# Six passes of a transformer kernel: seams between passes reordered, weights split by column halves, modulation partly moved into pass 0

## The reference

```
mod = silu(cond) @ Wmod + bmod               # block 0: 6 x 256 shifts and scales
h = LN(x) * (1 + sc1) + sh1;  x += attn(h @ Wqkv) @ Wos + bos          # pass 0
h = LN(x) * (1 + sc2) + sh2;  x += attn(h @ Wq, ctx @ Wk, ctx @ Wv) @ Woc + boc   # pass 1
h = LN(x) * (1 + sc3) + sh3;  x += gelu(h @ W1 + b1) @ W2 + b2         # pass 2
g = cond @ g_w + g_b, bt = cond @ b_w + b_b  # block 1: same for both norms
h = LN(x) * (1 + g1) + bt1;   x += attn(rope(h @ sa_wq), rope(h @ sa_wk), h @ sa_wv) @ sa_wo + sa_bo   # pass 3
h = LN(x) * (1 + g1) + bt1;   x += attn(rope(h @ ca_wq), rope(LN(ctx) @ ca_wk), LN(ctx) @ ca_wv) @ ca_wo + ca_bo   # pass 4
h = LN(x) * (1 + g2) + bt2;   x += gelu(h @ ff_w1 + ff_b1) @ ff_w2 + ff_b2   # pass 5
```

## Time and profile before

| what | us |
|---|---|
| median of 3 runs (4234.51 to 4236.21) | 4235.6 |
| the profiled execution | 4232.58 |
| its span | 4230.7 |
| TensorE matmuls busy | 4076.2 (96%) |
| VectorE busy | 2844.6 (67%) |
| ScalarE busy | 2746.4 (65%) |
| GpSimd busy | 2909.7 (69%) |

### The profile page before, as it was taken

The page is one execution under the profiler, slowest core; times in us unless marked ns, Lnnn a source line. Parts: engine busy times, 40 slices in busy tenths (PEclk is TensorE's granted clock), DMA queues, the critical chain, the costliest instruction groups (busy, mean ns, idle before and its releaser), DMA issues.

```text
span 4230.7 us, 95772 instructions
## 1 busy us (share of the span) xinstructions
PE 4076.2 (96%) x34870; PEld 3484.5 (82%) x34870; DVE 2844.6 (67%) x6058; ACT 2746.4 (65%) x10788; POOL 2909.7 (69%) x2714
## 2 busy tenths in 40 slices
PE   7999999999989999999999999999999999999999
PEld 6777777777779987888888888888888888888998
DVE  6888888888865556565656565777776767665443
ACT  5999999999953335666666666666666666664333
POOL 5777778888767775666565665666666666665776
PEclk9999999999999999999999999999999999999999
DMA  2110111111111212212121212322222222221110
GB/s 72 33 35 32 33 42 43 47 46 47 46 57 41 66 62 78 81 71 81 71 80 70 80 71 96 102 78 91 80 89 86 83 86 81 88 99 53 41 51 31
DMA packets 229270, 276.66 MB, mean 65 GB/s; under 512 B 37948, under 2 KB 160320, under 8 KB 228800
## 3 DMA queue, kind: packets, MB, share of 16 engines
q1 hardware_dynamic: 228732, 270.51, 18.8%
q10 hardware_dynamic: 68, 0.02, 0.0%
HBM read 85.89 MB, written 50.33 MB: 32 GB/s over the span
## 4 chain that ended last, share of the span: by engine, by line
PE 77%; POOL 10%; DVE 6%; ACT 4%; issue 3%; ACTq 0%; DMA 0%; SPq 0%; DVEq 0%; POOLq 0%
PE BANKS L580 18%; PE BANKS L582 16%; PE BANKS L581 16%; PE BANKS L768 7%; PE BANKS L732 7%; PE BANKS L720 6%; POOL PR L1194 3%; POOL Z L1236 3%; ACT PR L869 2%; PE BANKS L654 2%; PE BANKS L790 2%; POOL HL L1204 2%; DVE WL L1053 1%; POOL X L1250 1%; DVE PT L1016 1%
## 5 line engine op out<-in xcount | busy, mean ns | idle before, releaser
L1194 POOL TENSOR_TENSOR PR<-PR,RL 128x512 f32<-128x512 f32 x1024 | 1067.1, 1046 | 656.4 <-DVE RL L1021 655.8
L885 ACT ACTIVATE PR<-BANKS,NM 128x128 f32<-128x128 f32 x2048 | 729.0, 382 | 442.7 <-DVE NM L1067 440.5
L869 ACT ACTIVATE PR<-BANKS,NM 128x128 f32<-128x128 f32 x2048 | 728.4, 410 | 2.9 <-DVE NM L1009 2.8
L580 PE MATMUL BANKS<-HH,WH 128*128 128x512 f32 x1632 | 688.8, 422 | 6.4 <-DVE SN L1081 3.6
L768 PE MATMUL BANKS<-ID,PR 128*128 128x128 f32 x4096 | 624.7, 275 | 58.1 <-POOL PR L1194 28.3
L1067 DVE TENSOR_REDUCE NM<-BANKS 128x8 f32<-128x1024 f32 x256 | 313.2, 1224 | 490.8 <-PE BANKS L732 490.8
L581 PE MATMUL BANKS<-HL,WH 128*128 128x512 f32 x1632 | 643.0, 394 | 0.0
L582 PE MATMUL BANKS<-HH,WL 128*128 128x512 f32 x1632 | 642.0, 393 | 0.0
L768 PEld LDWEIGHTS BANKS<-ID,PR 128*128 128x128 f32 x4096 | 488.3, 140 | 184.0 <-POOL PR L1194 67.9
L869 ACT ACTIVATION_READ_ACCUMULATOR PR<-BANKS,NM 128x1 f32 x2048 | 514.2, 251 | 0.0
L1217 POOL TENSOR_TENSOR GL<-GF,GH 128x512 fp32r<-128x512 f32 x256 | 342.4, 1337 | 203.2 <-DVE GH L1165 203.2
(11 more groups left out here) (123 smaller groups left out, 10730.1 us busy)
## 6 DMA issues: line engine op xcount, KB each, us to landing
SW<-SN SPq DMA_DIRECT2D x1024, 128.0 KB, 2.1
x_scratch<-X SPq DMA_DIRECT2D x80, 512.0 KB, 3.2
X<-x_scratch SPq DMA_DIRECT2D x80, 512.0 KB, 4.0
CX<-in_ctx SPq DMA_DIRECT2D x32, 384.0 KB, 4.3
X<-in_x SPq DMA_DIRECT2D x16, 512.0 KB, 3.8
out<-X SPq DMA_DIRECT2D x16, 512.0 KB, 3.0
CX<-in_ctx SPq DMA_DIRECT2D x32, 128.0 KB, 4.4
STG<-in_L_xcond_W SPq DMA_DIRECT2D x4, 512.0 KB, 5.1
```

The lines of the kernel that those rows point to most:

```text
L580: e.matmul(o, lh, rh, start=first and i == 0, stop=False)
L869: made = e.activation(pr[:, r], bank[:, r], ACT.Exp, bias=nm[:, h:h + 1], accum_out=RL[npr(t)[0]][:, h:h + 1])
L885: made = e.activation(pr[:, r], bank[:, r], ACT.Exp, bias=nm[:, h:h + 1], accum_out=RL[npr(t)[0]][:, h:h + 1])
L1194: e.tensor_tensor(p3, p3, RL[npr(t)[0]][:, :].unsqueeze(2).broadcast_to([128, 4, 128]), ALU.mult).then_inc(s_nrm, 1)
```

## The change

The change has five parts.

- Prologue: modulation part 2 is made in pass 0, in two pieces of four columns at ticks TM = T0[0] + 1 and TM + 2, in bank 7, added at TM + 3 and applied at TM + 4 and TM + 5. `scores0` waits for parts 0 and 1 only, and copies to PT wait for part 2. Z of groups 0 and 1 is made on VectorE; group 1's statistics, root, Z and transposes stand at tg - 34, - 33, - 31 and from tg - 29 (before: from tg - 34, - 30, - 29 and - 24) and its Q products two ticks later. Wqkv is split one tick later.
- T0[2] and T0[5] are END[1] and END[4] (4 ticks less each), T0[3] is END[2] + 2 (one less).
- Feed forward buffers lie on AH, AL and ONES in pass 2 and on QT, KT, SN and the first V1 in pass 5. GELU waits for the last scores and not for the last transposes; exponentials of block 1 no longer wait for the end of pass 2, but `low` and V1 from the fourth on do.
- The four sums of `down` are pairs in two banks, (2, 3) for even groups and (6, 7) for odd ones. Group 1 of pass 2 is turned in banks 6 and 7.
- The weights sq, sk, sv, cq, ck, cv come by column halves of 512 with both row blocks, and products wait for their half alone. The splits of pass 4's weights stand in single ticks.

```diff
@@ T0, SOURCE
+TM = T0[0] + 1
-    T0[_p + 1] = END[_p] + {1: 4, 2: 3, 4: 4}.get(_p, 0)
+    T0[_p + 1] = END[_p] + {1: 0, 2: 2, 4: 0}.get(_p, 0)
+HALVES = ("sq", "sk", "sv", "cq", "ck", "cv")
@@ schedule
-            if kind == "a":
+            if (p, g) == (0, 1):
+                for b in range(G):
+                    at["stats", tg - 34].append(Batch(p, g, b))
+                    at["norm", tg - 31].append(Batch(p, g, b))
+                at["root", tg - 33].append((p, g))
+                turn = tg - 29
+            elif kind == "a":
...
+                    tq += 2 * ((p, g) == (0, 1))
...
-    chunks = [(T0[0] - 20, "Wqkv", 0), (T0[0] - 20, "Wqkv", 1)]
+    chunks = [(T0[0] - 19, "Wqkv", 0), (T0[0] - 19, "Wqkv", 1)]
...
-    chunks += [(e3 - 7, "cq", 0), (e3 - 7, "cq", 1), (e3 - 6, "ck", 0), (e3 - 6, "ck", 1), (e3 - 3, "cv", 0), (e3 - 3, "cv", 1),
-               (e3 + 5, "co", 0), (e3 + 5, "co", 1)]
+    chunks += [(e3 - 13, "cq", 0), (e3 - 12, "ck", 0), (e3 - 8, "cv", 0), (e3 - 6, "cq", 1), (e3 - 5, "ck", 1), (e3 - 2, "cv", 1),
+               (e3 - 1, "co", 0), (e3 + 6, "co", 1)]
@@ build: places
+            sb("HOLE0", [128, 2048], stack=first)
             AH = [sb(f"AH{i}", [128, 2, 512], R, stack=first) for i in range(2)]
             AL = [sb(f"AL{i}", [128, 2, 512], R, stack=first) for i in range(2)]
...
+            sb("HOLE1", [128, 5632], stack=gated)
+            GF[2] = [sb(f"GF{i}", [128, 512], stack=gated) for i in range(3)]
...
+        with gated2:
+            GF[5] = [sb(f"GF{i}_L1", [128, 512], stack=gated2) for i in range(3)]
@@ build: weights' old users, banks
-            w_free["cq", c] = (s_qk, 2 * 8 * NG - 1)
+            w_free["cq", c] = (s_qk, 2 * 8 * NG - 9 + 8 * c)
...
+        UP, TWO, THREE, FOUR, LATE, DOWN = (0, 1), (4, 5), (0, 1, 4), (4, 5, 6, 7), (6, 7), ((2, 3), (6, 7))
...
+            if tick == TM:
+                tp.add("modulation", (7,), s_mod, 3)
@@ SyncE
+                    if key in HALVES:
+                        name, k0 = PAIRED.get(key, (SOURCE.get(key), 0))
+                        k0 += 512 * c
+                        if key in CONTEXT:
+                            e.dma_start(stage[:, 0:512], a[name][0:128, k0:k0 + 512]).then_inc(ready, 16)
+                            e.dma_start(stage[0:64, 512:1024], a[name][128:CD, k0:k0 + 512]).then_inc(ready, 16)
+                            e.dma_start(stage[64:128, 512:1024], a[name][128:CD, k0:k0 + 512]).then_inc(ready, 16)
@@ TensorE
                 if tick == T0[0] - 20:
                     modulation(1)
-                    modulation(2)
+                if tick == TM:
+                    q.wait_ge(*tp.free("modulation"))
+                    modulation(2, 0)
+                if tick == TM + 2:
+                    modulation(2, 1)
...
-                    q.wait_ge(s_mod, 3)
+                    q.wait_ge(s_mod, 2)
...
-                    q.wait_ge(s_exp, NL0)
+                    q.wait_ge(s_exp, NL0 - 3 + min(j, 1))
...
-                        made = three(PS[(2, 3, 6, 7)[b]][:, 0:D], [(gh[:, s], gl[:, s], wh[:, j, :], wl[:, j, :])], j == 0, j == 7)
+                        made = three(PS[DOWN[g % 2][b // 2]][:, 256 * (b % 2):256 * (b % 2) + 256],
+                                     [(gh[:, s], gl[:, s], wh[:, j, :], wl[:, j, :])], j == 0 and b % 2 == 0, j == 7 and b % 2 == 1)
@@ ScalarE
-                    q.wait_ge(s_dn, 8 * NG)
+                    if m > 2:
+                        q.wait_ge(s_dn, 8 * NG)
...
-                    q.wait_ge(s_t, NL0 if p == 2 else 2 * NL0)
-                    e.activation(GF[f % 3][:, :], PS[tp.bank(("up", p, g, j))][:, :], ACT.Gelu, bias=col(WFF[p][2], j)).then_inc(s_gf, 1)
+                    q.wait_ge(*((s_s0, 16 * NG) if p == 2 else (s_s, 16 * NG)))
+                    e.activation(GF[p][f % 3][:, :], PS[tp.bank(("up", p, g, j))][:, :], ACT.Gelu, bias=col(WFF[p][2], j)).then_inc(s_gf, 1)
@@ VectorE
-                if tick == T0[0] - 11:
+                if tick == T0[0] - 12:
                     modulation(1)
+                if tick in (T0[0] - 5, T0[0] - 4):
+                    apply(tick - T0[0] + 6)
+                if tick == TM + 3:
                     modulation(2)
-                if T0[0] - 10 <= tick < T0[0] - 6:
-                    apply(tick - T0[0] + 11)
+                if tick in (TM + 4, TM + 5):
+                    apply(tick - TM - 1)
...
-                    if x.p < 2:
+                    if x.p < 2 and xq(x.p, x.g) > 1:
                         continue
```

More of the change, by code:

```diff
@@ L265, in build @@
         TB = sb("TB", [128, 4, D])
-        before, soft, gated, spare, first, second = (ExitStack() for _ in range(6))
+        before, soft, spare, first, gated, second, gated2 = (ExitStack() for _ in range(7))
         with before:
@@ L450, in build @@
                 if j == 0:
-                    for b in range(G):
-                        tp.add(("down", p, g, b), ((2, 3, 6, 7)[b],), s_res, 4 * xq(p, g) + b + 1)
+                    for i in range(2):
+                        tp.add(("down", p, g, i), (DOWN[g % 2][i],), s_res, 4 * xq(p, g) + 2 * i + 2)
         def h_of(p, g, context=False):
@@ L462, in col, with pieces, staged @@
             return COL[:, ROWS[name] + j:ROWS[name] + j + 1]
+        def pieces(buf, key, c):
+            if key in HALVES:
+                return wview(buf, key)[:, :, 512 * c:512 * c + 512]
+            rows, _, m, o = wchunk(key, c)
+            return buf[0:rows, o:o + m]
+        def staged(w, key, c):
+            rows, _, m, _ = wchunk(key, c)
+            if key in HALVES:
+                return STG[w % NSTG][:, :].rearrange("p (c n) -> p c n", c=2)
+            return STG[w % NSTG][0:rows, 0:m]
         def wchunk(key, c):
@@ L605, in project, with modulation @@
                 return e.matmul(o, HH[h][:, 1, s], wl[:, 1, cols], start=False, stop=True)
-            def modulation(part):
+            def modulation(part, half=None):
                 first, end = PARTS[part]
-                for m in range(first, end):
+                bank = PS[part if part < 2 else tp.bank("modulation")]
+                for m in range(first, end) if half is None else range(first + 4 * half, first + 4 * half + 4):
                     if m < 12:
@@ L619, in modulation @@
                         q.wait_ge(s_wgb, 64)
-                    o = PS[part][:, NB * (m - first):NB * (m - first) + NB]
+                    o = bank[:, NB * (m - first):NB * (m - first) + NB]
                     e.matmul(o, ls[0], rhs[:, 0, :], start=True, stop=False)
                     made = e.matmul(o, ls[1], rhs[:, 1, :], start=False, stop=True)
-                made.then_inc(s_mod_mm, 1)
+                if half != 0:
+                    made.then_inc(s_mod_mm, 1)
             q.wait_ge(s_ident, 16)
@@ L819, in _ @@
                         q.wait_ge(s_exp, NL0)
[L820 to L821 removed]
+                        for i in range(2):
+                            q.wait_ge(*tp.free(("down", p, g, i)))
                     for b in range(G):
                         s = slice(128 * b, 128 * b + 128)
[L824 removed]
+                        made = three(PS[DOWN[g % 2][b // 2]][:, 256 * (b % 2):256 * (b % 2) + 256],
+                                     [(gh[:, s], gl[:, s], wh[:, j, :], wl[:, j, :])], j == 0 and b % 2 == 0, j == 7 and b % 2 == 1)
                     made.then_inc(s_dn, 1)
@@ L938, in _ @@
                         q.wait_ge(*w_free[key, c])
-                    e.activation(WH[0:rows, o:o + m], STG[w % NSTG][0:rows, 0:m], ACT.Copy).then_inc(s_whi, 1)
+                    e.activation(pieces(WH, key, c), staged(w, key, c), ACT.Copy).then_inc(s_whi, 1)
         @block.vector
@@ L951, in modulation @@
                 bias = COL[:, ROWS["bmod"] + first:ROWS["bmod"] + end] if part < 2 else COL[:, ROWS[L1 + "g1_b"]:ROWS[L1 + "g1_b"] + 8]
-                e.tensor_tensor(MOD[:, first:end, :], PS[part][:, 0:NB * (end - first)].rearrange("p (m b) -> p m b", b=NB),
+                bank = PS[part if part < 2 else tp.bank("modulation")]
+                e.tensor_tensor(MOD[:, first:end, :], bank[:, 0:NB * (end - first)].rearrange("p (m b) -> p m b", b=NB),
                                 bias.unsqueeze(2).broadcast_to([128, end - first, NB]), ALU.add).then_inc(s_mod, 1)
```

77 lines of the change are left out of this document (34 added, 43 removed).

## The result

The kernel after takes 4216.5 us (median of 5 runs, 4214.0 to 4219.2); the kernel before, on the same chip, 4234.5. The ratio is 0.9960 (95% interval 0.9949 to 0.9971): faster by about 18 us, where 40 were forecast, and outside the range of 4180 to 4214. The first line is the page's busy time by engine, the others are busy time by stage as in the earlier trace rows (length, busy us and instructions of each engine, granted clock), the seams in stretches of nearly equal work before and after.

A forecast was written before the change was run, and what follows sets the result against it. TensorE and ScalarE were both taken as nearly full in passes 0 and 1, TensorE alone as the bound from 1610 us. 11 + 9 + 4 + 6 + 10 = 40 us gave 4195.6 us, range 4180 to 4214.

The forecast's parts named there:

- Its own sign of being wrong: Passes 0 and 1 over 3 us longer between first and last exponential, or a new several-us wait at an up or PV.
- Prologue: Start of the kernel: first exponential 14 us earlier, at 43, less 3 given back in pass 0; 11 us gained (4.9 to 15).
- the share given back: Pass 0: cost of modulation part 2, its addition and sets moved there, taken as 3 us (bounds nothing to 9.1).
- Seam 1/2: Between passes 1 and 2: four ticks less and earlier up products overlap the seam; 9 us gained (4 to 14).
- Seam 2/3: Between passes 2 and 3: one tick less puts the maximum ahead of two `so` splits; 4 us gained (1.5 to 6.6).
- Seam 3/4: Between passes 3 and 4: single splits hide and products wait only for their half; 6 us gained (2 to 9).
- Seam 4/5: Between passes 4 and 5: four ticks less, hidden state's transposes earlier where ScalarE has room; 10 us gained (5 to 14.7).
- (b): Rival at the seams: overlap works half, GELU chain or transposes' banks hold TensorE, clock falls again; 4210 us, chance 0.09.
- (c): Rival on VectorE: Z slowed beside GpSimd's normalization, up to 1.42 us against 0.41; 4200 us, chance 0.08.
- (d): Rival in pass 0: modulation pieces leave TensorE's clock at its lower level, 7.4 us more per batch; slower, chance 0.03.
- (e): Rival: ups wait for something ending only with pass 1, pass 0 eats the prologue's gain; no change, chance 0.03.
- (f): Rival: modulation products run at the upper clock level, part 1 taking 3.3 instead of 6.7 us; 4191 us, chance 0.04.

The follow-up runs named there:

- e8: Kernel after with modulation part 2, its addition and sets back in the prologue behind part 1; 4223.9 us, ratio 0.9971.
- e5: Kernel after with the second modulation piece, the addition and sets 3 and 4 one tick earlier; 4216.2 us over four scattered runs, ratio 0.9958.
- e1: Kernel after with the four ticks of pass 2 put back (T0[2] = END[1] + 4); 4220.1 us, ratio 0.9971.
- e13: Kernel after with statistics and Z of group 0 of passes 2 and 5 on 16 of 256 columns; 4216.2 us, one run.
- e14: Kernel after with ScalarE copying only one of four batches of group 0's hidden state per half in passes 2 and 5; 4215.3 us, one run.
- e6: Kernel after with Z of groups 0 and 1 of pass 2 on GpSimd instead of VectorE; 4223.0 us, ratio 0.9972.
- e10: Kernel after with the hidden state of pass 2's group 0 made earlier and piece by piece inside pass 1; 4217.4 us, ratio 0.9961.
- e12: Kernel after with second modulation piece and addition one tick earlier, spare banks and single splits at 2/3, group 0's chain earlier, f1 and f2 spread; 4212.5 us.
- e7: Kernel after with pass 3's first two Q and K products in banks 4 and 5 and the `so` splits two and four ticks later; 4213.0 us.
- e2: Kernel after with the tick of pass 3 put back (T0[3] = END[2] + 3); 4212.0 us, ratio 0.9954.
- e16: Kernel after with second modulation piece and addition one tick earlier, T0[3] = END[2] + 3, and T0[5] = END[4] + 2; 4210.1 us.
- e4: Kernel after with the second modulation piece one tick earlier (TM + 1 instead of TM + 2); 4215.2 us, ratio 0.9959.

## Why the prediction was wrong

Its own sign of being wrong came. From the first exponential to the last one of pass 1 it takes 1145.12 us for 1133.00 before: 12.1 longer, where it set 3 as the limit. Of these 6.4 lie ahead of tile 16, 5.1 in D, 0.6 between. The first down product stands at 1200.69 for 1193. So work moved into passes 0 and 1 was priced too low where it lands. At 2/3 and 4/5 other steps failed, as said below.

**Prologue: -7.5 for -11.** The first exponential (43.23 for 43) was right within its scatter (41.6 to 44.1 over the kernels without e8), the share given back (6.4 for 3) mis-sized, and the text held its cause: "the copies to PT wait for that addition, and what takes bank 7 next, with TensorE's queue behind it". I took 3, "since only the second piece meets a busy queue", and never asked what the addition itself is queued behind: a split that waits for ScalarE's exponentials. e5 removes just that and has -10.9. That this is the forecast's 11 is luck. The 3 were meant for the modulation, and of the 6.4 only some 3.5 are: 3.3 for the place of the addition, hardly anything for the rest. The other 2.8 are given back without any modulation in pass 0 (e8). Group 1's Q products, which I moved from the prologue behind the first scores and never charged, are the likely cause; no run moves them alone. The moved products are still worth 4.4 (e8).

**Seam 1/2: -3.2 for -9.** This step failed in kind. I listed what VectorE gets "before the end of pass 1", left out ScalarE's copies of the hidden state, and gave the work ahead of the last exponential no price of its own, though the earlier trace rows say both TensorE and ScalarE are busy 92% there. e1 gives the account: 5.1 us paid ahead of the last exponential, 7.3 won behind it. Counted from tile 496, the delay against e1 is 2.3 us at tile 504, 3.9 at 506, 6.9 at 509 and 5.1 from 510 on. Of the 5.1, 1.4 come back when VectorE's share is short (e13), 0.2 with ScalarE's (e14), 0.5 with Z elsewhere (e6), and with an earlier place none in e10 and 1.2 in e12. TensorE's clock alone does not carry it (e7). What carries the rest stays open: the transposes on TensorE and their banks are the work left, and were not tried alone.

**Seam 2/3: +2.8 for -4.** Only the sign of the wait for the exponential was right (3.0 for 4.87). The step "one tick less puts the maximum ahead" forgot that the first Q and K products move as well, into a ring of banks (0, 1, 4) that the last up products share. e2 and e7 show it from two sides.

**Seam 3/4: -4.6 for -6**, with scatter from -4.3 to -5.8: within its bounds of 2 to 9. The mechanism shows in the waits: two for SN of 3.6 us together and one of 2.3 for KT in the kernel before are 0.5, 0.6 and 1.2 after, and the clock reads 1.00 from 2690 to 2720 where it was 0.53 in the earlier trace rows. No run undoes this part alone.

**Seam 4/5: -4.6 for -10.** I called idle and clock "recoverable" together, 9.0 + 5.7 us. The clock's part came, 3.7 us in the busy time; the idle part did not, 8.8 us of 9.0 stayed: "the transposes now come four ticks earlier, where ScalarE has room" was wrong. ScalarE's queue still held one of PV's two waits (2.2 us, 0.9 in e14), and half of the overlap does as well as all (e16).

**The rivals.** (b), the overlap half working at 4210, was nearest, for the reason given ("the transposes' banks hold TensorE"), though idle time rather than the clock remained. (c) did not show: Z took 0.35 us each in the prologue and 0.7 at the seam, as before. (d) fell: behind the first exponential the clock was at its lower level from 46 to 60 us, not on end. (e) fell: P and the seams 1/2, 3/4 and 4/5 all gained. (f) came true for part 1 in this one profile and brought nothing: it ran at the upper level, yet Q waited 2.69 us for GpSimd's HL and started at 24.82; in e4, where it took the lower level as I had forecast, Q started at 24.85. The five terms were taken from inside their bounds, yet three of them came out below the lower one (3.2 under 4, -2.8 under 1.5, 4.6 under 5): the bounds themselves left out what moved work costs where it lands.

## What to carry to other kernels

Moving work across a seam into a stage that is 92% busy was a trade here, not a gain: price what it costs where it lands, and undo each tick alone, since one here lost what it was to save. Where a moved result frees a bank or buffer, follow the engine that frees it back through its own queue; one addition behind one weight split cost 3.3 us. Starting other work earlier took hardly any idle time from these seams; what it won at 4/5 came with a higher granted clock. And when several edits differ in one place, kernels with the same code in a piece tell its scatter, and a stretch between two instructions behind the change says more than one from the start.
